# Probabilities times context in f16 high and low parts, with rows transposed and copied in pairs

## The reference, cut to what matters

```
kv_rope = kv_c * cos + rotate_half(kv_c) * sin
scores = einsum('bshr,bhlr->bhsl', q_r, k_r)
attn = softmax(scores)
ctx_c = einsum('bhsl,bld->bhsd', attn, kv_rope)     # the product that is changed
out = einsum over heads of ctx_c with w_kc_kv, then @ Wo.T
```

## Time and profile before

| | |
|---|---|
| median of 3 runs | 796.93 us (795.12 to 796.94) |
| profiled execution | 801.42 us, its span 799.6 us |
| PE busy | 658.0 us, 82% |
| DVE busy | 418.3 us, 52% |
| ACT busy | 288.8 us, 36% |
| POOL busy | 291.6 us, 36% |
| L1200, the product that is changed | 512 matmul records, 78.3 us busy |

### The profile page before, as it was taken

How to read it: one execution, slowest core, us unless ns; L and a number is a source line. 1 busy time by engine, 2 the same in 40 slices (tenths; PEclk the granted TensorE clock), 3 DMA queues, 4 the chain that set the end, 5 groups by cost and what they waited for, 6 DMA issues and landing times.

```text
span 799.6 us, 16264 instructions
## 1 busy us (share of the span) xinstructions
PE 658.0 (82%) x6210; PEld 535.2 (67%) x6210; DVE 418.3 (52%) x1098; ACT 288.8 (36%) x798; POOL 291.6 (36%) x279
## 2 busy tenths in 40 slices
PE   6977676889999999899999999999865088888840
PEld 5866455767786786786886886786745077777730
DVE  1135455255477577476567666666653223333325
ACT  1112355134535445435445436336131033333310
POOL 4004376421211531431431431400303337777760
PEclk9565555789999999999999999999998579999985
DMA  8954998699300100200200200100101179999978
GB/s 231 289 99 115 214 212 165 182 306 333 104 1 2 70 19 2 82 7 2 81 7 2 83 6 2 67 2 2 64 2 50 38 188 294 298 286 299 304 112 262
DMA packets 105227, 97.61 MB, mean 122 GB/s; under 512 B 32526, under 2 KB 99088, under 8 KB 105152
## 3 DMA queue, kind: packets, MB, share of 16 engines
q1 hardware_dynamic: 86160, 78.21, 34.7%
q0 software_dynamic: 12288, 17.95, 10.5%
q10 hardware_dynamic: 6704, 0.42, 0.6%
HBM read 62.32 MB, written 35.19 MB: 122 GB/s over the span
## 4 chain that ended last, share of the span: by engine, by line
PE 53%; DVE 13%; issue 10%; DMA 8%; POOL 7%; ACT 5%; SPq 2%; ACTq 2%; POOLq 0%; DVEq 0%; PEldq 0%
PE bank L1134 7%; PE bank L1136 6%; PE bank L1135 6%; POOL expert_sums L543 6%; PE bank L1200 5%; PE bank L1168 4%; PE bank L1153 4%; PE bank L1189 4%; DMA expert_sums<-Wh,etok 4%; PE bank L1237 3%; PE bank L1182 3%; PE bank L1111 2%; PE bank L1181 1%; DVE qspace L823 1%; PE bank L1123 1%
## 5 line engine op out<-in xcount | busy, mean ns | idle before, releaser
L543 POOL DMA_INDIRECT expert_sums<-Wh,etok x64 | 98.8, 1545 | 39.4 <-issue 22.6
L486 POOL DMA_INDIRECT expert_rows<-h,slot x64 | 62.6, 978 | 85.1 <-DVE slot L920 68.0
L610 ACT ACTIVATE pr<-bank,nmax 128x257 f32<-128x257 f32 x128 | 61.1, 477 | 85.5 <-DVE nmax L829 84.1
L1134 PE MATMUL bank<-space,Wh 128*128 128x128 f16 x512 | 89.1, 221 | 2.5 <-DVE space L866 1.5
L1135 PE MATMUL bank<-space,Wh 128*128 128x128 f16 x512 | 88.9, 220 | 0.0
L1136 PE MATMUL bank<-space,Wl 128*128 128x128 f16 x512 | 88.8, 220 | 0.0
L1200 PE MATMUL bank<-Cr,pT 128*128 128x64 f32 x512 | 78.3, 280 | 5.6 <-DVE On L839 4.5
L469 POOL TENSOR_TENSOR Cr<-C,Ct 128x192 f32<-128x192 f32 x64 | 38.7, 628 | 114.6 <-PE bank L1200 112.4
L1200 PEld LDWEIGHTS bank<-Cr,pT 128*128 128x128 f32 x512 | 74.4, 210 | 7.1 <-issue 6.0
L829 DVE TENSOR_REDUCE nmax<-bank 128x1 f32<-128x257 f32 x128 | 53.4, 419 | 42.5 <-PE bank L1182 40.3
L618 ACT COPY pT<-bank 128x256 f32<-128x256 f32 x128 | 47.5, 371 | 69.4 <-PE bank L1189 68.3
(11 more groups left out here) (172 smaller groups left out, 1396.6 us busy)
## 6 DMA issues: line engine op xcount, KB each, us to landing
ring<-L_ffn_gate_up_proj_dram SPq DMA_DIRECT2D x64, 192.0 KB, 4.1
expert_rows<-h SPq DMA_DIRECT2D x8, 1284.0 KB, 17.4
Wh<-expert_rows SPq DMA_DIRECT2D x64, 160.5 KB, 5.0
ring<-L_ffn_down_proj_dram SPq DMA_DIRECT2D x64, 96.0 KB, 5.0
expert_sums<-h SPq DMA_DIRECT2D x4, 1152.0 KB, 13.4
Wl<-expert_sums SPq DMA_DIRECT2D x16, 256.0 KB, 5.5
C<-ctx_dram SPq DMA_DIRECT2D x24, 128.0 KB, 3.2
space<-L_xattn_Wo_dram SPq DMA_DIRECT2D x8, 256.0 KB, 4.7
```

The lines of the kernel that those rows point to most:

```text
L486: e.indirect_dma_start(XE[:, :], bass.IndirectOffsetOnAxis(ap=slot[:, k:k + 1], axis=0), h3[:, :], None, bounds_check=E * CAP - 1, oob_is_ ...
L543: e.indirect_dma_start(Y[n % NY][:, :], bass.IndirectOffsetOnAxis(ap=etok[:, n % 4:n % 4 + 1], axis=0), ye[:, n % 4], None, bounds_check=Y ...
L610: e.activation(pr[:, s, :], bank[r % 2][:, 0:NL], ACT.Exp, bias=nmax[:, s:s + 1], accum_out=rsum[:, s:s + 1]).then_inc(expd, 1)
L1134: e.matmul(dst, ah, bh, start=first and n == 0, stop=False)
```

## The change

The product of probabilities and context is done in f16: both operands are split into a high and a low part, and three products (high x high, high x low, low x high) replace each f32 one, so six f16 matmuls a row. The rows are transposed in pairs into the whole of bank 2, at odd steps; ACT copies the pair to pTh (f16) in one instruction and DVE makes pTl as bank 2 minus pTh in one more (`pt_low`), placed right behind `max_row`. POOL makes two more arrays a batch: Crs high (a sum written in f16) and Crs low (Cr minus Crs high). The sums move one step later (row r at step r + 4), `normalise` to steps 7, 11, 15, 19; parts of X_AT and BEHIND move one step later too, and there are 22 steps. BEHIND has nothing at steps 15, 18 and 21, X_AT nothing at 15. The lines that change, without their surroundings:

```diff
@@ -32,8 +32,8 @@
-X_AT = {2: ["kt1"], 6: ["kt2"], 7: ["cT0"], 10: ["kt3"], 11: ["cT1"], 15: ["cT2", "hT"], 16: ["qa"], 18: ["qb"],
-        19: ["cT3", "kt0"], 20: ["out"]}
+X_AT = {2: ["kt1"], 6: ["kt2"], 8: ["cT0"], 10: ["kt3"], 12: ["cT1"], 16: ["cT2", "hT"], 17: ["qa"], 18: ["qb"],
+        20: ["cT3", "kt0"], 21: ["out"]}
@@ -41,9 +41,10 @@
-          15: ["pv0"], 16: ["pv1"], 17: ["pv2"], 18: ["pv3"]}
+          16: ["pv0"], 17: ["pv1"], 19: ["pv2"], 20: ["pv3"]}
-STEPS = ROWS + 5
+STEPS = ROWS + 6
+PAIRS = ROWS // 2
@@ -120,7 +121,9 @@
-        pT = sb("pT", [P, 2, 2, P])
+        pTh = sb("pTh", [P, 2, 2, 2, P], f16)
+        pTl = sb("pTl", [P, 2, 2, 2, P], f16)
+        Crs = sb("Crs", [P, BT, 2, 2, DC], f16)
@@ -234,6 +237,7 @@
+        c_split, pt_high = sem("c_split"), sem("pt_high")
@@ -362,7 +366,7 @@
-            e.wait_ge(roped, 2 * BT)
+            e.wait_ge(roped, 3 * BT)
@@ -389,7 +393,7 @@
-                e.wait_ge(roped, i * (2 * BT))
+                e.wait_ge(roped, i * (3 * BT))
@@ -465,13 +469,16 @@
+                e.tensor_tensor(Crs[:, b, :, 0], C[:, b, 0:2], Ct[:, b, 0:2], ALU.add).then_inc(roped, 1)
+                e.wait_ge(roped, i * (3 * BT) + 3 * b + 2)
+                e.tensor_tensor(Crs[:, b, :, 1], Cr[:, b, 0:2, 0, :], Crs[:, b, :, 0], ALU.subtract).then_inc(c_split, 1)
-                e.wait_ge(roped, i * (2 * BT) + 2 * b + 2)
+                e.wait_ge(roped, i * (3 * BT) + 3 * b + 3)
@@ -610,12 +617,12 @@
-            def copy_row(i, r):
-                e.wait_ge(transposed, i * ROWS + r + 1)
-
-                if r >= 2:
-                    e.wait_ge(summed, i * ROWS + r - 1)
-                e.copy(pT[:, r % 2], bank[2][:, 0:2 * P].rearrange("p (c t) -> p c t", c=2)).then_inc(pt_ready, 1)
+            def copy_pair(i, k):
+                e.wait_ge(transposed, i * PAIRS + k + 1)
+
+                if k >= 2:
+                    e.wait_ge(summed, i * ROWS + 2 * k - 2)
+                e.copy(pTh[:, k % 2], bank[2][:, :].rearrange("p (n c t) -> p n c t", n=2, c=2)).then_inc(pt_high, 1)
@@ -659,8 +666,8 @@
-                        if 2 <= r <= ROWS + 1:
-                            copy_row(i, r - 2)
+                        if r % 2 and 3 <= r <= ROWS + 1:
+                            copy_pair(i, r // 2 - 1)
@@ -828,6 +835,13 @@
+            def pt_low(i, k):
+                e.wait_ge(pt_high, i * PAIRS + k + 1)
+                if k >= 2:
+                    e.wait_ge(summed, i * ROWS + 2 * k - 2)
+                e.tensor_tensor(pTl[:, k % 2], bank[2][:, :].rearrange("p (n c t) -> p n c t", n=2, c=2), pTh[:, k % 2],
+                                ALU.subtract).then_inc(pt_ready, 1)
+
@@ -953,7 +967,9 @@
-                        if r % RB == 2 and r > RB:
+                        if r % 2 and 3 <= r <= ROWS + 1:
+                            pt_low(i, r // 2 - 1)
+                        if r % RB == 3 and r > RB:
@@ -1181,23 +1197,28 @@
-            def transpose_row(i, r):
-                e.wait_ge(expd, i * ROWS + r + 1)
-
-                e.wait_ge(pt_ready, i * ROWS + r)
-                for c in range(2):
-                    ins = e.transpose(bank[2][:, c * P:(c + 1) * P], pr[:, r % (2 * RB), c * P:(c + 1) * P], ident[:, :])
+            def transpose_pair(i, k):
+                e.wait_ge(expd, i * ROWS + 2 * k + 2)
+
+                e.wait_ge(pt_ready, i * PAIRS + k)
+                for n in range(2):
+                    for c in range(2):
+                        o = 2 * P * n + P * c
+                        ins = e.transpose(bank[2][:, o:o + P], pr[:, (2 * k + n) % (2 * RB), c * P:(c + 1) * P], ident[:, :])
-                e.wait_ge(pt_ready, i * ROWS + r + 1)
+                e.wait_ge(pt_ready, i * PAIRS + r // 2 + 1)
+                    e.wait_ge(c_split, i * BT + b + 1)
-                    ins = e.matmul(bank[3][:, o:o + DC], pT[:, r % 2, c, :], Cr[:, b, c, 0, :], start=c == 0, stop=c == 1)
+                    e.matmul(bank[3][:, o:o + DC], pTh[:, r // 2 % 2, r % 2, c, :], Crs[:, b, c, 0, :], start=c == 0, stop=False)
+                    e.matmul(bank[3][:, o:o + DC], pTh[:, r // 2 % 2, r % 2, c, :], Crs[:, b, c, 1, :], start=False, stop=False)
+                    ins = e.matmul(bank[3][:, o:o + DC], pTl[:, r // 2 % 2, r % 2, c, :], Crs[:, b, c, 0, :], start=False, stop=c == 1)
@@ -1281,10 +1302,10 @@
-                        if 2 <= r <= ROWS + 1:
-                            transpose_row(i, r - 2)
-                        if 3 <= r <= ROWS + 2:
-                            sum_row(i, r - 3)
+                        if r % 2 and 3 <= r <= ROWS + 1:
+                            transpose_pair(i, r // 2 - 1)
+                        if 4 <= r <= ROWS + 3:
+                            sum_row(i, r - 4)
```

## The result

The changed kernel takes 871.08 us (median of 4, 869.99 to 871.52), the kernel before in the same study 796.69 (median of 4, 795.12 to 796.94): a ratio of 1.0927, 95% interval 1.0877 to 1.0977. The profiled execution has a span of 869.5 us against 799.6, 69.9 more. The forecast was 838 with a range up to 866: the sign is right, the loss is 74 us instead of 41. Executions some per cent above the others of their kernel aren't counted as fast ones: 820.84 and 826.67 us of four in e6, and 848.52 of four in e10, which is the one profiled there.

A forecast was written before the change was run, and what follows sets the result against it. PE was taken to set a tile's pace, DVE next. Tile losses of 36.6 us plus 5 for the clock made 42, taking the span from 799.6 to 841, or 838 us on the median's level; range 790 to 866, likeliest case 812 to 866.

The forecast's parts named there:

- The product, 0.18 a row: Sums on PE: six f16 matmuls 0.03 us apart take 0.18 us a row, instead of 0.39 for four f32 records.
- Steps 4 to 9: Steady tile: PE waits 0.8, 0.7 and 0.2 us; step 9 at 363.1 instead of 362.81, the gain of seven rows gone.
- Steps 10 to 12: Steady tile: normalise ends late, PE idles 2.5 us at step 12; step 13 starts 2.0 us late.
- Step 15: Steady tile: PE idles 3.5 us before row 12's sum, waiting for cast, subtraction and normalise.
- Steps 16 to 21: End of a steady tile: PE idles 2.9 us before cT3 instead of 1.57; from step 15's start 20.8 us instead of 16.65.
- 5.6 us for each steady tile: Steady tiles: the next tile starts at 401.8 instead of 396.18; five tiles, 2 to 6, give 28 us.
- The clock, 3 x 1.7 = 5: Ends of tiles: a clock of 0.50 in about half of the tiles, 1.7 us each, 5 us in all.
- The second rival: Every tile: half clock behind both idle times, 3.4 x 7 instead of 5, so 857 us; chance above 866 0.06.
- Tile 1, 1.6: Tile 1: early rows keep about 2.5 us of their gain against 4.15 lost at its end, 1.6 us more.
- Tile 0, 2: Tile 0: its end 4 us longer, rows at half clock somewhat cheaper, 2 us more.
- PE stays the bound: Whole kernel: DVE's idle takes up the subtractions, sums leave 0.265 us a row; faster, about 771 us; chance 0.16.
- Gain and idle cancel: Steady tiles: gain up to step 15 offsets loss behind it, 797 to 805 us; chance 0.06 for within 0.3%.

The follow-up runs named there:

- e6: The changed kernel without the low part of the probabilities: no subtraction on DVE, four f16 matmuls a row; 804.32 and 807.27 us.
- e10: The changed kernel without the low part, with a DVE instruction of the subtraction's size in its place that PE doesn't wait for; 839.14 us, 1.0536.
- e3: The changed kernel's pairs, steps and order with the f32 product of before, no subtraction on DVE; 835.64 us, 1.0475.
- e1: The changed kernel with 36, 44 and 42 more bf16 matmuls filling PE's idle times at steps 12, 16 and 20; 848.0 us, 1.0612.
- e9: The kernel before, rows one by one in the old order, four f16 matmuls a row, no low part of the probabilities, no subtraction; 781.65 us, 0.9831.
- e4: The kernel before with the six-matmul f16 product alone: rows transposed, cast and subtracted one by one, old steps; 823.19 us, 1.0351.
- e2: The changed kernel with normalise ahead of the subtraction on DVE at steps 7, 11, 15 and 19; 846.37 us, 1.060.
- e7: The changed kernel with the four pv products back at steps 15 to 18 instead of 16, 17, 19, 20; 868.58 us, 1.0922.
- e5: The kernel before with one more DVE instruction of 0.69 us at eight odd steps a tile, which only DVE waits for; 805.43 us, 1.0108.
- e8: The kernel before with a batch's first sum waiting only for the first of normalise's three instructions; 796.15 us, 1.0024.
- e11: The changed kernel with normalise ahead of the subtraction and 30, 34 and 42 filling bf16 matmuls at steps 12, 16, 20; 825.13 us, 1.0393.

## Why the forecast had the sign and missed the size

The chain of attribution by measured times: 797 before; pairs and later sums, old product 836 (+39); four f16 matmuls for it 806 (-30); DVE's load 839 (+33); the subtraction in the chain and the two other matmuls 871 (+32). In the old order: four f16 matmuls 782 (-15), subtraction and the two others 823 (+41). Each step holds its share of the clock, and of what differs ahead of tile 1 without a known cause. So here are the profiled executions by parts, as in the first table; the last column estimates how much of tiles 2 to 6 ran at a clock of 0.50 (twice the length times what the clock lacks of 1.00):

| kernel | to tile 1 | tile 1 | tiles 2 to 6 | tile 7 | rest | at 0.50 |
|---|---|---|---|---|---|---|
| before | 150.4 | 64.7 | 294.2 | 54.6 | 235.6 | 4 |
| e3, pairs, f32 | 150.7 | 72.1 | 329.0 | 55.4 | 232.2 | 33 |
| e6, pairs, four matmuls | 138.6 | 65.6 | 311.5 | 54.5 | 232.3 | 30 |
| e10, e6 and DVE's load | 152.8 | 68.4 | 334.5 | 58.5 | 232.4 | 58 |
| changed | 156.8 | 75.7 | 344.2 | 60.3 | 232.6 | 55 |
| e1, changed, filled | 160.3 | 71.9 | 323.5 | 59.5 | 236.4 | 0 |
| e9, old order, four | 140.0 | 61.9 | 289.4 | 52.6 | 236.8 | 14 |
| e4, old order, six | 149.6 | 70.3 | 305.6 | 59.5 | 233.9 | 4 |

e1 prices the last column: 55 us at 0.50 cost 20.8. By that, some 11 of the 34.8 us that pairs and later sums cost in tiles 2 to 6 are the clock, and some 10 of the 23.0 of DVE's load, but none of the 9.7 of the subtraction's place.

- *The product, 0.18 a row.* Right: 0.03 from start to start, six in a row. The Trainium skill, "TensorE: Matmul & The Clock Gate", section "Back-to-back issue gap", has both figures; the trace agrees with the floor of about 25 ns and not with the 62. Four transposes take 0.49 us (420.18 to 420.67), forecast 0.45. The saving of 34 us for a PE that alone decides looks like what e3 to e6 gave, 30, for two matmuls fewer; 12 of these 30 lie ahead of tile 1, 17.5 in tiles 2 to 6, where the clock is much the same.
- *Steps 4 to 9.* Right in sum: 0.52 for on_ready before row 4's sum (forecast 0.7), 0.45 for q2's bank before k0 (0.8), none before k1 (0.2), and 1.03 before q0, which wasn't forecast. Counted from the tile's first scores, step 9 starts 0.6 us later than before (forecast 0.3).
- *Steps 10 to 12.* Right: idle 2.38 (forecast 2.5).
- *Step 15.* Right in kind: idle 3.03 (forecast 3.5), with ACT's second spread and v3 ahead of the cast as the walk had it. But step 15 starts 3.1 us later than before, not 1.5: steps 12 and 13 run in part at half clock. e2 leaves 2.43 with normalise taken out.
- *Steps 16 to 21.* 2.84 before cT3 (forecast 2.9). But from step 15's start to the next tile's first scores it is 443.33 - 419.76 = 23.6 instead of 20.8: the idle times are as walked, and what lies between them runs at half clock.
- *5.6 us for each steady tile.* About right at full clock. e1's tiles 2 to 6 take 323.45. The kernel before takes 294.2, of which 1.7 are the fall of the earlier trace rows; that makes 292.5 at full clock: 30.9 over five tiles, 6.2 each.
- *The clock, 3 x 1.7 = 5.* This is the step that failed. The term allowed one fall in every other tile, and only at the tile's end; there are two or three in each, behind the idle times at steps 12 and 16 and before cT3 (2.38, 3.03 and 2.84 us in the tile shown), and they cost 20.8 us in five tiles, 4.2 each. The second rival had the mechanism with two falls a tile, 3.4 us, at 857; its chance beyond the range was put at 0.06. The same page of the Trainium skill, section "A second HAM failure mode: psum-queue depth-cycling", says that brief idle times between groups of matmuls make the clock fall and rise again and again; the trace agrees, with falls behind 13 of 15 in five tiles. The single 0.50 before, behind only 1.57 us, spoke for it more than I let it.
- *Tile 1, 1.6.* Wrong: 10.9. The early rows keep no gain. About 3.4 is the clock (e1 has 71.85, its stop of PE 0.44 shorter). Another 3.96 us is one stop of PE, at the end of which nothing shown was waited for:

```profile
202.72 0.80 PE L1207 MATMUL bank<-ident,pr 128*128 128x128 f32 x3 [3.96 <-issue]
```

  It stands in the changed kernel, e1 (3.52), e2 (4.00), e4 (4.61) and e7 (3.88), all with six f16 matmuls a row, and not in the kernel before, e3, e5, e6, e8, e9 and e10; in e11, which also has six, PE stops for 2.11 us amid the filling matmuls. In each of the six the DMA share is 1.06 to 1.09 and a transfer of the instruction queue (q8 on the page) lies in the stop, in e11 in the 0.3 us ahead of it. That PE waits for its next instructions behind the other transfers would fit; no run tests it.
- *Tile 0, 2.* It was 6.4. The end of this part lies between 138.6 and 160.3 us in the kernels of this study with no order that I can explain; it goes at the pace of the weights. The profiled execution of e8 differs from the one of before by 0.1 us or less in every later part, and by 6.3 in this one (144.2 against 150.4). Open.
- *PE stays the bound.* It does not: PE is busy 57.27 of 68.58 us. *Gain and idle cancel*: not even in e6, where the subtraction is gone; its 806 look like it, but tiles 2 to 6 are 17.3 us longer than before and the part ahead of tile 1 is 11.8 shorter.

The sum again, with the measured terms: 6.4 + 10.9 + 50.0 + 5.6 - 3.0 = 69.9. By spans the forecast of 42 was 28 us short: in tiles 2 to 6 the clock 14.1 (20.8 less the 1.7 that the kernel before has too, against 5) and the walk 2.9 (30.9 against 28), tile 1 9.3, tile 0 4.4, tile 7 0.6, and the experts -3.0. The other 5 of the 33 between the medians are nearly all the level: the profiled execution of before lay 4.5 above its median, the changed kernel's 0.4 above its own.

## What to carry to other kernels

When a change puts a step into a chain that PE waits for, walk one tile instruction by instruction; then count each new idle time of over 2 us on PE twice, once for itself and once for the clock behind it (here 1.5 us each, behind 13 of 15). A busy share of 39 in 58 us on DVE is no room: a load of 5.5 us a tile cost 6.4 us over five tiles in one order and 23.0 in another. Try the product in the old order first, and without the part that needs the second engine, if its precision can be spared: with four matmuls it won 15 us there, with six it lost 26, and 74 with pairs and later sums on top. Compare such kernels part by part: a stretch that goes at the pace of the weights moved by up to 22 us from one to the next and made totals fit that didn't.

## What the runs showed of the hardware

- f16 matmuls of 64 columns, each with its own 128-column weights, start 0.03 us apart in runs of six at a granted clock of 1.00, and 0.05 to 0.06 apart at 0.50 (203.38 to 203.59).
- Between short transposes and sums the granted clock fell to 0.50 (1.2 GHz) behind 13 of 15 idle times of 2.38 to 3.82 us in tiles 2 to 6 of the changed kernel, and came back within 4 us, twice after about 7. Behind 1.57 us it fell in one of six tiles of the kernel before, behind 1.48 us in four of six of e9. With the idle times filled by small bf16 matmuls it stayed at 1.00 (2.4 GHz) in six tiles, waits of 1.02 and 0.41 us included.
- A wait for a semaphore can be named "issue"; the end of the instruction on the other engine, 0.1 us earlier, shows what it was.
